# A later slot for the normalisations of the second mixing stage in a decoder layer on one NeuronCore

## The chip, the core and the metric

The kernel runs on one core of a Trainium2 chip, as a single launch. The metric is the device time of one execution in microseconds (us). The engines are TensorE (PE, with its weight loads shown apart as PEld), VectorE (DVE), ScalarE (ACT), GpSimd (POOL) and the queue of SyncE (SP). Each executes its own instructions in order and waits for the others on semaphores.

## The reference, cut to what matters

The layer is self-attention, a cross-attention block that mixes along the sequence (an attention-free transformer with a local bias), and a quantised feed-forward network, over x of shape (4, 1024, 512) in float32. The change lies in the second half of the cross block, from the weighted sums to the first layer norm:

```
def _aft_local(emb, wq, bq, wk, bk, wv, bv, wo, bo, pos_bias):
    ...
    num = jnp.einsum('tj,bjd->btd', ew, ek * v)
    den = jnp.einsum('tj,bjd->btd', ew, ek)
    y = jax.nn.sigmoid(q) * num / den
    return y @ wo + bo
...
attn = _aft_local(emb, wq, bq, wk, bk, wv, bv, wo, bo, pos_bias)
a = _layer_norm(attn + emb, gamma, beta)
```

with `_layer_norm(x) = (x - mu) * rsqrt(var + 1e-5) * gamma + beta` over the last axis of 512.

## The kernel before, in words

The layer is written as six stages one after the other, each with its own memory and semaphores: `project_qkv`, `attend`, `mix_in`, `mix_out`, `cross_ffn`, `quantised_ffn`. The change touches only `mix_out`, the second mixing stage, which the trace shows from about 1905 to 2275 us.

`mix_out` goes over B = 4 batches ("blocks"), each of T = 1024 tokens in TB = 8 tiles of 128 rows. A block is worked in 8 slots, `for s in range(TB)`, and every engine has a `body(b, first, more)` that lists what it does in each slot. The first and the last block are written out, the two between are a loop. In slot s:

- TensorE turns the y of two slots ago (`turn_y`, L1637), turns one of the two parts of a tile of exponentials two tiles ahead (`turn_e`, L1619), makes the denominator and the numerator of tile s (`weigh`, L1652 for the far part and L1658 for the near one; called den and num), turns the second part, and multiplies the y of tile s-2 by the output weights (`out_product`, L1681). Each product is split in high and low parts. In slot 7 it also turns the sums of the next block (L1628), ahead of the out product.
- ScalarE copies the turned tiles into their high parts (`round_y` L1728, `round_e` L1715 and L1716).
- GpSimd makes the low parts of the exponentials (`split_e`, L1567, two in a slot). A finished half is multiplied by gamma and shifted by beta there as well (`scale_and_shift`, L1575 and L1577, a pair for each of its four tiles), and its store to `a_rows` is issued from there (L1581).
- VectorE makes the low part of y (`split_y`, L1762), then `divide` (L1770, the reciprocal L1773, y itself L1776), then the `residual` of tile s-3 (L1788) and its statistics (L1790).

A half is four tiles, so a block has two: half 0 is tiles 0 to 3, half 1 tiles 4 to 7. The residual of a half's last tile comes in slot 6 (half 0) and in slot 2 of the next block (half 1). It is followed by the means and variances (L1795), the reciprocal square roots in 14 small instructions on all four tiles together (lines 114 to 119), and the four normalisations in place, `(z - mean) * rstd` (L1802). The last half of all has a path of its own (`finish_last`). After the last block two more slots (8 and 9) drain the out products, and slot 10 the last residual.

The accumulator has four banks in a ring. `free_bank` says what each product waits for before it writes its bank: den of slot s takes the bank that the out product of slot s-2 wrote, and that one is read by the residual of slot s-1.

```
                        for kind in ("den", "num"):
                            weigh(b, s, kind)
                        if ahead:
                            turn_e(*ahead, 1)
                        if more and s == TB - 1:
                            turn_sums(b + 1)
                        if not (first and s < LAG):
                            out_product(b, s)
```

The diff's functions are printed here.

Of the kernel before, what the change touches and what calls it, by code (L numbers as in the profile page):

```python
# [27 lines left out]
ALU = mybir.AluOpType  # L28
# [4 lines left out]
B, T, D = 4, 1024, 512  # L33
# [6 lines left out]
HT = HALF // P  # L40
# [29 lines left out]
def past(engine, sem, value):  # L70

    if not (isinstance(value, int) and value <= 0):
        engine.wait_ge(sem, value)


def half_of(rows, n):

    return rows.rearrange("(n t p) d -> n p t d", p=P, t=HT)[bass.ds(n, 1)].rearrange("a p t d -> p (a t) d")
# [7 lines left out]
def row(vector, start, n):  # L86

    return vector[start:start + n].rearrange("(a n) -> a n", a=1).to_broadcast([P, n])
# [1310 lines left out]
def mix_out(nc, ident, ewT_parts, e0_rows, wo, gamma, beta, emb_rows, expq_rows, ek_cols, ekv_cols, sum_cols, a_rows):  # L1399
# [11 lines left out]
    ACC, LAG = 4, 2  # L1411
    AHEAD = 2
    STEPS = 2 * HT + RSQRT_STEPS
    with ExitStack() as ctx:
# [22 lines left out]
        z = sb("z", [P, 2, HT, D])  # L1437
        w_raw = z[:, 0]
        stats = sb("stats", [P, HT, 6])
        moments = sb("moments", [P, HT, 2])  # L1440
        rstd = sb("rstd", [P, HT])
# [26 lines left out]
        norm_ready = sem("norm_ready")  # L1468
# [15 lines left out]
        def bank_of(kind, t):  # L1484

            step = t + (LAG if kind == "out" else 0)
            return (len(KINDS) * step + KINDS.index(kind)) % ACC
# [7 lines left out]
        with nc.Block() as block:  # L1495
# [50 lines left out]
            @block.gpsimd  # L1546
            def _(pool):
                pool.dma_start(gamma_row[:, :], row(gamma, 0, D)).then_inc(rows_loaded, 16)
                pool.dma_start(beta_row[:, :], row(beta, 0, D)).then_inc(rows_loaded, 16)

                pool.memset(zero[:, :], 0.0).then_inc(setup_step, 1)
                pool.memset(sums_wide[:, :, :, :, :], 0.0).then_inc(setup_step, 1)
                pool.wait_ge(setup_step, 2)

                def widen_sums(b):

                    pool.wait_ge(sums_loaded, (b + 1) * 16)
                    past(pool, sums_turned, b * 2)
                    for i in range(3):
                        pool.tensor_tensor(sums_wide[:, :, :, i, 0:TB], sums_in[:, :, :, :], zero[:, :].to_broadcast([P, 2 * KB * TB])  # L1560
                                           .rearrange("p (i c t) -> p i c t", i=2, c=KB), ALU.add).then_inc(sums_copied, 1)

                def split_e(b, t, i):
                    k = (b * TB + t) * 2 + i + 1
                    pool.wait_ge(e_full_ready, k)
                    pool.wait_ge(e_hi_ready, k)
                    pool.tensor_tensor(e_lo[:, t, i], e_full[:, i], e_hi[:, t, i].bitcast(F32), ALU.subtract).then_inc(e_lo_ready, 1)  # L1567

                def scale_and_shift(b, h, tiles):

                    n = b * 2 + h
                    for t in tiles:
                        i = n * HT + t
                        pool.wait_ge(norm_ready, i + 1)
                        pool.tensor_tensor(z[:, h, t], z[:, h, t], gamma_row[:, :], ALU.mult).then_inc(scaled, 1)  # L1575
                        pool.wait_ge(scaled, i + 1)
                        pool.tensor_tensor(z[:, h, t], z[:, h, t], beta_row[:, :], ALU.add).then_inc(shifted, 1)  # L1577
                    if HT - 1 in tiles:
                        pool.wait_ge(shifted, (n + 1) * HT)
                        pool.sem_inc(wait_taken, 1)  # L1580
                        pool.dma_start(half_of(a_rows, n), z[:, h]).then_inc(stored[h], 16)  # L1581

                def body(b, first, more):
                    for s in range(TB):
                        ahead = block_ahead(b, s, more)
                        if ahead:
                            split_e(*ahead, 0)
                            split_e(*ahead, 1)

                        if s == 0 and not first:  # L1590
                            scale_and_shift(b - 1, 0, range(2, HT))
                        if s in (3, 4) and not first:
                            scale_and_shift(b - 1, 1, range(2 * (s - 3), 2 * (s - 2)))
                        if s == 5 and more:
                            widen_sums(b + 1)
                        if s == 7:
                            scale_and_shift(b, 0, range(2))

                widen_sums(0)
                for t in range(2):  # L1600
                    for i in range(2):
                        split_e(0, t, i)
                pool.wait_ge(rows_loaded, 32)
                sequences(pool, body)
                scale_and_shift(B - 1, 0, range(2, HT))
                pool.wait_ge(norm_ready, N // P)
                pool.sem_inc(wait_taken, 1)
                pool.dma_start(half_of(a_rows, 2 * B - 1), z[:, 1]).then_inc(stored[1], 16)
                for h in range(2):
                    pool.wait_ge(stored[h], B * 16)  # L1610
# [142 lines left out]
            def _(dve):  # L1753
# [10 lines left out]
                def divide(b, t):  # L1764

                    i = b * TB + t
                    dve.wait_ge(expq_loaded[t % 4], (b * 2 + t // 4 + 1) * 16)
                    past(dve, read["num"], i)
                    dve.wait_ge(ready["den"], i + 1)
                    dve.scalar_tensor_tensor(out=recip[:, :], in0=expq_in[:, t % 4], scalar=1.0, in1=acc[:, bank_of("den", t)],  # L1770
                                             op0=ALU.add, op1=ALU.mult).then_inc(read["den"], 1)
                    dve.wait_ge(read["den"], i + 1)
                    dve.reciprocal(recip[:, :], recip[:, :]).then_inc(recip_step, 1)  # L1773
                    dve.wait_ge(recip_step, i + 1)
                    dve.wait_ge(ready["num"], i + 1)
                    dve.tensor_tensor(y[:, t % 4], acc[:, bank_of("num", t)], recip[:, :], ALU.mult).then_inc(read["num"], 1)  # L1776

                def residual(b, t):

                    if t < 0:  # L1780
                        b, t = b - 1, t + TB
                    i, h, k = b * TB + t, t // HT, t % HT
                    s0 = (b * 2 + h) * STEPS
                    if k == 0:
                        past(dve, stored[h], b * 16)
                    dve.wait_ge(emb_loaded[t % 4], (b * 2 + t // 4 + 1) * 16)
                    dve.wait_ge(ready["out"], i + 1)
                    dve.tensor_tensor(z[:, h, k], acc[:, bank_of("out", t)], emb_in[:, t % 4], ALU.add).then_inc(read["out"], 1)  # L1788
                    dve.wait_ge(read["out"], i + 1)
                    dve.bn_stats(stats[:, k], z[:, h, k]).then_inc(stat_step, 1)  # L1790
                    if k == HT - 1:
                        dve.wait_ge(stat_step, s0 + HT)
                        dve.sem_inc(wait_taken, 1)
                        for j in range(HT):
                            dve.bn_aggr(moments[:, j], stats[:, j]).then_inc(stat_step, 1)  # L1795
                        dve.wait_ge(stat_step, s0 + 2 * HT)
                        rsqrt(dve, moments[:, :, 1], rstd[:, :], nt_half[:, :], nt_square[:, :], stat_step, s0 + 2 * HT)
                        if isinstance(i, int) and i == N // P - 1:
                            finish_last(h)
                        else:  # L1800
                            for j in range(HT):
                                dve.tensor_scalar(z[:, h, j], z[:, h, j], moments[:, j, 0:1], rstd[:, j:j + 1],  # L1802
                                                  ALU.subtract, ALU.mult).then_inc(norm_ready, 1)

                def finish_last(h):

# [8 lines left out]
                def body(b, first, more):  # L1815
                    for s in range(TB):
                        if not (first and s < LAG):
                            split_y(b, s - LAG)
                        if first and s == 1:
                            dve.wait_ge(w_hi_ready, 1)  # L1820
                            dve.tensor_tensor(w_lo[:, :, :], w_raw, w_hi[:, :, :].bitcast(F32), ALU.subtract).then_inc(w_lo_ready, 1)
                        divide(b, s)
                        if more and s == TB - 1:
                            split_sums(b + 1)
                        if not (first and s <= LAG):
                            residual(b, s - LAG - 1)
# [842 lines left out]
```

## Time and profile before

| what | value |
|---|---|
| median of 3 runs | 3545.81 us (3543.29 to 3549.79) |
| the profiled execution's own time | 3542.34 us |
| its span | 3540.7 us |
| TensorE busy | 3167.0 us, 89% of the span |
| VectorE busy | 2344.0 us, 66% |
| ScalarE busy | 1767.6 us, 50% |
| GpSimd busy | 1171.8 us, 33% |

The profile is of one execution. Its span is the time from the first to the last instruction that it shows; the execution's own time holds the launch around it too. A busy share is an average over all six stages, so what a change in one stage is worth is read from that stage. Start times are in us from the start of the span.

### The profile page before, as it was taken

The numbers are of one execution on the slowest core, as the hardware profiler recorded it, in microseconds if no ns is written. First come the engines' busy times: TensorE is split into PE (matmuls) and PEld (weight loads), VectorE is DVE, ScalarE is ACT, GpSimd is POOL, SyncE is SP. The second block draws the span as 40 slices with busy tenths as digits, with TensorE's granted clock in tenths as the row PEclk, the third lists the DMA queues.
The fourth block names the chain that finished last, engine by engine and source line by source line (L and its number), as shares of the span: only waits on it lengthen the run. The fifth ranks groups of instructions, "written<-read, shape, count | busy, mean of one in ns | idle before, by whom it ended". The sixth has DMA issues, their size and how long they took to land. (4 is left out here: it accounts for less than half of the span.)

```text
span 3540.7 us, 57138 instructions
## 1 busy us (share of the span) xinstructions
PE 3167.0 (89%) x19234; PEld 2282.3 (64%) x19234; DVE 2344.0 (66%) x4197; ACT 1767.6 (50%) x3130; POOL 1171.8 (33%) x901
## 2 busy tenths in 40 slices
PE   6998999999999999789996998599999999368886
PEld 5776666666666666567775777487877788334443
DVE  5562788888888888644553888634445444379996
ACT  3331888888888888522323222132222222076662
POOL 2343311312231132144442455300111111058886
PEclk9999999999999999999998999799999999689999
DMA  6775311321222122355645443321111110201112
GB/s 216 239 243 169 85 60 56 92 62 56 73 79 61 56 85 68 122 181 188 228 171 184 129 131 118 108 84 42 42 42 43 42 42 29 82 22 55 60 42 72
DMA packets 239351, 350.53 MB, mean 99 GB/s; under 512 B 31792, under 2 KB 129104, under 8 KB 239184
## 3 DMA queue, kind: packets, MB, share of 16 engines
q1 hardware_dynamic: 208256, 290.41, 25.5%
q0 software_dynamic: 8912, 32.82, 2.8%
q10 hardware_dynamic: 22016, 25.17, 2.0%
q8 instruction: 93, 1.52, 0.2%
q14 instruction: 74, 0.61, 0.1%
HBM read 210.68 MB, written 137.64 MB: 98 GB/s over the span
## 5 line engine op out<-in xcount | busy, mean ns | idle before, releaser
L887 DVE CUSTOM_DVE_ANT_0 attend_scores<-attend_scores,attend_bias_table 128x1024 f32<-128x1024 f32 x512 | 630.5, 1232 | 164.8 <-PE attend_scores L741 161.5
L814 ACT ACTIVATE attend_probs<-attend_scores,attend_neg_max 128x1024 f32<-128x1024 f32 x512 | 571.7, 1117 | 141.0 <-DVE attend_neg_max L887 131.3
L753 PE MATMUL attend_turned<-ident,attend_probs 128*128 128x128 f32 x4096 | 557.3, 275 | 12.6 <-DVE attend_probsT L895 12.5
L753 PEld LDWEIGHTS attend_turned<-ident,attend_probs 128*128 128x128 f32 x4096 | 472.9, 141 | 121.4 <-DVE attend_probsT L895 30.2
L741 PE MATMUL attend_scores<-attend_k_stack,attend_q_stack 96*128 96x512 f32 x1024 | 373.4, 446 | 18.1 <-DMA attend_q_stack<-qk_parts 15.0
L822 ACT COPY attend_probsT<-attend_turned 128x512 f32<-128x512 f32 x640 | 359.5, 583 | 24.7 <-PE attend_turned L753 23.1
L2217 DVE TENSOR_TENSOR cross_ffn_h_lo<-cross_ffn_hidden,cross_ffn_h_hi 128x512 fp32r<-128x512 f32 x128 | 95.8, 753 | 363.7 <-ACT cross_ffn_h_hi L2114 363.1
L703 POOL TENSOR_TENSOR attend_out_parts<-attend_out_full,attend_out_parts 128x256 fp32r<-128x256 f32 x64 | 46.6, 727 | 847.3 <-ACT attend_out_parts L829 847.3
L768 PE MATMUL attend_out_acc<-attend_probsT,attend_v_in 128*32 128x256 f32 x4096 | 312.9, 389 | 0.7 <-DVE attend_out_full L905 0.7
L741 PEld LDWEIGHTS attend_scores<-attend_k_stack,attend_q_stack 96*128 96x128 f32 x1024 | 154.1, 190 | 175.2 <-issue 154.8
L895 DVE COPY attend_probsT<-attend_turned 128x512 f32<-128x512 f32 x384 | 263.5, 686 | 1.3 <-PE attend_turned L753 1.3
L2111 ACT ACTIVATE cross_ffn_hidden<-cross_ffn_h_acc,cross_ffn_b_cols 128x512 f32<-128x512 f32 x128 | 88.2, 689 | 266.3 <-PE cross_ffn_h_acc L2028 250.1
L697 POOL TENSOR_TENSOR attend_bias_table<-attend_neg_distance,attend_slope_now 128x1920 f32<-128x1920 f32 x64 | 214.8, 3388 | 1.4
L2026 PE MATMUL cross_ffn_h_acc<-cross_ffn_aT_hi,cross_ffn_w_hi 128*128 128x512 f32 x512 | 203.6, 398 | 5.6 <-issue 5.6
L2375 POOL TENSOR_TENSOR quantised_ffn_conv<-quantised_ffn_conv,quantised_ffn_right_tap 128x512 f32<-128x512 f32 x128 | 178.4, 1394 | 88.8 <-DVE quantised_ffn_conv L2543 88.8
L2039 PE MATMUL cross_ffn_out_acc<-cross_ffn_w_hi,cross_ffn_h_hi 128*128 128x512 f32 x512 | 206.3, 403 | 1.1 <-DVE cross_ffn_h_lo L2217 0.6
L2027 PE MATMUL cross_ffn_h_acc<-cross_ffn_aT_hi,cross_ffn_w_lo 128*128 128x512 f32 x512 | 202.9, 396 | 0.0
L2114 ACT CAST cross_ffn_h_hi<-cross_ffn_hidden 128x512 fp32r<-128x512 f32 x128 | 79.5, 621 | 247.1 <-PE cross_ffn_out_acc L2041 246.1
L2028 PE MATMUL cross_ffn_h_acc<-cross_ffn_aT_lo,cross_ffn_w_hi 128*128 128x512 f32 x512 | 202.5, 396 | 0.0
L2040 PE MATMUL cross_ffn_out_acc<-cross_ffn_w_lo,cross_ffn_h_hi 128*128 128x512 f32 x512 | 202.3, 395 | 0.0
L2041 PE MATMUL cross_ffn_out_acc<-cross_ffn_w_hi,cross_ffn_h_lo 128*128 128x512 f32 x512 | 202.3, 395 | 0.0
L2381 POOL TENSOR_TENSOR quantised_ffn_h_scaled<-quantised_ffn_h,quantised_ffn_scale_row 128x512 f32<-128x512 f32 x128 | 164.2, 1285 | 12.3 <-ACT quantised_ffn_scale_row L2513 7.6
(294 smaller groups left out, 6644.5 us busy)
## 6 DMA issues: line engine op xcount, KB each, us to landing
qk_parts<-qkv_qk_out SPq DMA_DIRECT2D x64, 512.0 KB, 3.2
attend_k_stack<-qk_parts SPq DMA_DIRECT2D x192, 128.0 KB, 2.5
attend_q_stack<-qk_parts SPq DMA_DIRECT2D x192, 128.0 KB, 2.7
qkv_wq_raw<-L_ffn_w POOLq DMA_DIRECT2D x16, 1024.0 KB, 7.6
o_parts<-attend_out_parts ACTq DMA_DIRECT2D x64, 256.0 KB, 2.5
carried_o_in<-o_parts SPq DMA_DIRECT2D x32, 512.0 KB, 6.5
qkv_x_in<-x SPq DMA_DIRECT2D x8, 1024.0 KB, 5.7
v_rows<-qkv_v_out SPq DMA_DIRECT2D x32, 256.0 KB, 3.4
```

The lines of the kernel that those rows point to most:

```text
L697: pool.tensor_tensor(bias_table[:, h], neg_distance[:, :], slope_now[:, h:h + 1].to_broadcast([P, SPAN]), ALU.mult).then_inc(table_ready, 1)
L741: last = pe.matmul(scores[:, i % 2, k * HALF:(k + 1) * HALF], q_stack[:, h, queries], k_stack[:, h, k * HALF:(k + 1) * HALF], start=True, ...
L753: last = pe.transpose(turned[:, x, c], probs[:, i % 2, k * P:(k + 1) * P], ident[:, :])
L768: last = pe.matmul(out_acc[rows, 0:QG], v_in[:, c, rows], probsT[:, (qg - 1) % 2, c, h], start=(c == 0), stop=(c == TB - 1))
L814: act.activation(probs[:, i % 2], scores[:, i % 2], ACT.Exp, bias=neg_max[:, i % 4:i % 4 + 1], scale=-1.0, accum_out=den[:, qg % 2, j, h:h ...
L822: act.copy(probsT[:, qg % 2, x * HB:(x + 1) * HB, h, j * P:(j + 1) * P], turned[:, x]).then_inc(copied[x], 1)
L887: dve.tensor_tensor_reduce(scores[:, i % 2], scores[:, i % 2], bias_table[:, h, at:at + T], -1.0, BIG, ALU.add, ALU.min, neg_max[:, i % 4: ...
L895: dve.tensor_copy(probsT[:, qg % 2, HB:TB, h, j * P:(j + 1) * P], turned[:, 1]).then_inc(copied[1], 1)
L2026: pe.matmul(out, w1_hi[:, c, cols], aT_hi[:, c], start=c == 0, stop=False)
L2027: pe.matmul(out, w1_lo[:, c, cols], aT_hi[:, c], start=False, stop=False)
L2028: last = pe.matmul(out, w1_hi[:, c, cols], aT_lo[:, c], start=False, stop=c == KB - 1)
L2039: pe.matmul(out_acc[:, t], hi, w2_hi[:, j], start=j == 0, stop=False)
```

## The change

Three things move inside `mix_out`; no instruction is added or taken out, and no tile changes its size.

- VectorE: the four normalisations of a half leave `residual` and become `normalise(h)`. It is called a slot later, after `divide` and before the residual: in slot 7 for half 0 (`HT + LAG + 1`), in slot 3 of the next block for half 1 (`LAG + 1`).
- GpSimd: the scale and shift of half 0 is done two tiles in slot 0 and two in slot 1 of the next block (before: two in slot 7 and two in slot 0), that of half 1 in slots 4 and 5 (before: 3 and 4). The store of a half follows its last pair. After the last block all four tiles of half 0 are done in one go (before: two).
- GpSimd: the sums of the next block are widened in slot 6 (before: slot 5).

```
@@ gpsimd, body @@
-                        if s == 0 and not first:
-                            scale_and_shift(b - 1, 0, range(2, HT))
-                        if s in (3, 4) and not first:
-                            scale_and_shift(b - 1, 1, range(2 * (s - 3), 2 * (s - 2)))
-                        if s == 5 and more:
+                        if s in (0, 1) and not first:
+                            scale_and_shift(b - 1, 0, range(2 * s, 2 * s + 2))
+                        if s in (4, 5) and not first:
+                            scale_and_shift(b - 1, 1, range(2 * (s - 4), 2 * (s - 3)))
+                        if s == 6 and more:
                             widen_sums(b + 1)
-                        if s == 7:
-                            scale_and_shift(b, 0, range(2))
...
-                scale_and_shift(B - 1, 0, range(2, HT))
+                scale_and_shift(B - 1, 0, range(HT))
@@ vector, residual @@
                         if isinstance(i, int) and i == N // P - 1:
                             finish_last(h)
-                        else:
-                            for j in range(HT):
-                                dve.tensor_scalar(z[:, h, j], z[:, h, j], moments[:, j, 0:1], rstd[:, j:j + 1],
-                                                  ALU.subtract, ALU.mult).then_inc(norm_ready, 1)
+
+                def normalise(h):
+
+                    for j in range(HT):
+                        dve.tensor_scalar(z[:, h, j], z[:, h, j], moments[:, j, 0:1], rstd[:, j:j + 1],
+                                          ALU.subtract, ALU.mult).then_inc(norm_ready, 1)
@@ vector, body @@
                         divide(b, s)
+                        if s == HT + LAG + 1:
+                            normalise(0)
+                        if s == LAG + 1 and not first:
+                            normalise(1)
                         if more and s == TB - 1:
                             split_sums(b + 1)
                         if not (first and s <= LAG):
                             residual(b, s - LAG - 1)
```

## Rows read from the trace of the kernel before

**Rows 1.** The page: busy time of each engine, share of the span, instructions.

```profile
PE 3167.0 (89%) x19234; PEld 2282.3 (64%) x19234; DVE 2344.0 (66%) x4197; ACT 1767.6 (50%) x3130; POOL 1171.8 (33%) x901
```

**Rows 2.** Waits of TensorE, 1925 to 2275 us: who for whom, us, times, longest.

```profile
PE mix_out_acc L1681 <- DVE mix_out_yT_lo L1762: 25.2, 9, 4.9
PE mix_out_acc L1652 <- DVE mix_out_z L1788: 7.8, 6, 1.5
```

**Rows 3.** Timeline of TensorE, a block's end: start, us, instruction [idle before it].

```profile
2087.27 0.50 PE L1681 MATMUL mix_out_acc<-mix_out_w_hi,mix_out_yT_hi 128*128 128x512 f32 x1 [3.98 <-DVE mix_out_yT_lo L1762]
...
2091.73 0.60 PE L1637 MATMUL mix_out_turned<-ident,mix_out_y 128*128 128x128 f32 x4
...
2094.21 0.47 PE L1652 MATMUL mix_out_acc<-mix_out_sums,mix_out_e_stack 96*128 96x512 f32 x1 [1.45 <-DVE mix_out_z L1788]
```

**Rows 4.** Timeline of TensorE, a block's middle, and den of its slot 6.

```profile
2126.08 0.50 PE L1681 MATMUL mix_out_acc<-mix_out_w_hi,mix_out_yT_hi 128*128 128x512 f32 x1 [1.63 <-DVE mix_out_yT_lo L1762]
...
2128.98 0.60 PE L1637 MATMUL mix_out_turned<-ident,mix_out_y 128*128 128x128 f32 x4
...
2131.39 0.50 PE L1652 MATMUL mix_out_acc<-mix_out_sums,mix_out_e_stack 96*128 96x512 f32 x1 [1.37 <-DVE mix_out_z L1788]
...
2148.95 0.48 PE L1652 MATMUL mix_out_acc<-mix_out_sums,mix_out_e_stack 96*128 96x512 f32 x1
```

**Rows 5.** Timeline of VectorE: a block's end, a block's middle, the last block's end.

```profile
2082.77 3.85 DVE L1802 TENSOR_SCALAR mix_out_z<-mix_out_z,mix_out_moments,mix_out_rstd 128x512 f32<-128x512 f32 x4
...
2091.24 0.69 DVE L1776 TENSOR_TENSOR mix_out_y<-mix_out_acc,mix_out_recip 128x512 f32<-128x512 f32 x1
...
2123.52 1.91 DVE L1802 TENSOR_SCALAR mix_out_z<-mix_out_z,mix_out_moments,mix_out_rstd 128x512 f32<-128x512 f32 x4
2125.35 0.68 DVE L1762 TENSOR_TENSOR mix_out_yT_lo<-mix_out_turned,mix_out_yT_hi 128x512 fp32r<-128x512 f32 x1
...
2130.66 0.68 DVE L1788 TENSOR_TENSOR mix_out_z<-mix_out_acc,mix_out_emb_in 128x512 f32<-128x512 f32 x1
...
2240.12 3.80 DVE L1802 TENSOR_SCALAR mix_out_z<-mix_out_z,mix_out_moments,mix_out_rstd 128x512 f32<-128x512 f32 x4
```

**Rows 6.** Timeline of GpSimd: a split in slot 0, two behind a store.

```profile
2094.17 1.29 POOL L1567 TENSOR_TENSOR mix_out_e_lo<-mix_out_e_full,mix_out_e_hi 128x512 fp32r<-128x512 f32 x1 [3.84 <-ACT mix_out_e_hi L1716]
...
2146.13 2.55 POOL L1567 TENSOR_TENSOR mix_out_e_lo<-mix_out_e_full,mix_out_e_hi 128x512 fp32r<-128x512 f32 x2
```

**Rows 7.** Instructions of L1802: ns minimum, median, maximum; first and last start.

```profile
L1802 DVE TENSOR_SCALAR mix_out_z<-mix_out_z,mix_out_moments,mix_out_rstd x28: 539/546/1530, 2003.3 to 2242.4; 128x512 f32<-128x512 f32 x28
```

**Rows 8.** Windows: length, busy per engine, granted clock of PE, DMA share, GB/s.

```profile
2083.00:2093.00 10.00, 5.78 (x23) 4.28 (x21) 9.90 (x10) 2.06 (x6) 6.50 (x5) 0.83 0.00 0
3156.00:3164.00 8.00, 4.62 (x24) 2.48 (x25) 7.05 (x14) 5.26 (x11) 4.36 (x4) 1.00 0.01 2
3252.00:3260.00 8.00, 6.51 (x34) 3.54 (x35) 7.97 (x15) 5.27 (x11) 4.86 (x4) 1.00 0.21 68
3301.00:3309.00 8.00, 6.03 (x23) 3.20 (x24) 6.42 (x13) 3.70 (x7) 3.19 (x4) 0.79 0.21 66
1531.00:1537.00 6.00, 5.84 (x18) 4.69 (x19) 5.58 (x16) 0.69 (x1) 2.93 (x3) 0.69 0.38 129
```

**Rows 9.** Timeline of TensorE: gaps in three stages (the number in brackets).

```profile
1531.15 0.77 PE L1186 MATMUL mix_in_acc<-mix_in_eT_hi,mix_in_wk_hi 128*128 128x512 f32 x1 [6.40 <-DVE mix_in_x L1329]
...
2251.20 0.50 PE L1681 MATMUL mix_out_acc<-mix_out_w_hi,mix_out_yT_hi 128*128 128x512 f32 x1 [1.58 <-DVE mix_out_yT_lo L1762]
...
3157.93 0.63 PE L2420 MATMUL quantised_ffn_turned<-ident,quantised_ffn_h 128*128 128x128 f32 x4 [3.09 <-DVE quantised_ffn_block_max L2551]
...
3206.14 0.63 PE L2420 MATMUL quantised_ffn_turned<-ident,quantised_ffn_h 128*128 128x128 f32 x4 [3.60 <-DVE quantised_ffn_block_max L2551]
...
3302.97 1.09 PE L2420 MATMUL quantised_ffn_turned<-ident,quantised_ffn_h 128*128 128x128 f32 x4 [3.60 <-DVE quantised_ffn_block_max L2551]
...
3449.37 0.83 PE L2420 MATMUL quantised_ffn_turned<-ident,quantised_ffn_h 128*128 128x128 f32 x4 [3.60 <-DVE quantised_ffn_block_max L2551]
```

## The prediction

> **What bounds the kernel now.** I read the page first: TensorE (PE) is busy 3167.0 of 3540.7 us [rows 1], so a stage can gain only where PE stands still in it. Next come PE's waits in the second mixing stage, 1925 to 2275 us: the largest is the out product (L1681) held for y's low part from DVE (L1762), 25.2 us in 9 waits; the next that recurs is the first weigh product of a slot (L1652) held for the residual (L1788), 7.8 us in 6 waits [rows 2]. Third, the timelines of PE and DVE show that both sit where a half is normalised. I follow one block end and one block middle; the first, second and third blocks have such an end, the second to fourth such a middle, and the last half 0 (in the last block's slot 7) runs into the stage's tail.
>
> *Block end (slot 7, half 0).* PE waits 3.98 us, starts the out product at 2087.27, turns y for the next slot at 2091.73, waits 1.45 us and starts den(0) at 2094.21 [rows 3]. *Block middle (slot 3, half 1).* 1.63 us of wait, out product at 2126.08, turn at 2128.98, 1.37 us, den(4) at 2131.39 [rows 4]. DVE is idle in neither: it ends its reciprocal square roots and runs the four normalisations, split_y, divide and the residual without a break [rows 5]. So DVE's queue from the square roots to the residual of the next slot sets when den(0) and den(4) may start. In the code this is free_bank: den of slot s writes the bank that out of slot s-2 held, which the residual of slot s-1 on DVE reads.
>
> **The change, part by part.**
>
> *Normalisations moved behind divide.* They stay ahead of the residual of the same slot. Call the square roots' end R. Before: R, four normalisations, split_y, divide, residual, den. After: R, split_y, divide, four normalisations, residual, den. The same instructions stand between R and den. The out product does start earlier: split_y begins at R instead of R+1.83 (2123.52 to 2125.35) in the middle, and instead of R+3.77 at a block end (the four last 3.85 there against 1.91, and the next instruction starts 0.08 before they end) [rows 5]. PE starts 0.73 behind split_y's start (2125.35 to 2126.08 [rows 4, 5]), so at a block end at 2082.77+0.73=2083.5, where it was ready at 2087.27-3.98=2083.29. But PE then only comes sooner to den and waits there for the same residual. I book nothing for the wait that goes: what is late next is den. The wait becomes one piece. At a block end the out product (2.90 us at full clock, 2126.08 to 2128.98 [rows 4]) ends at 2086.4, the turns take 1.04 (2131.39-1.37-2128.98), and PE stands from 2087.4 until den. In the middle PE was ready for the out product at 2126.08-1.63=2124.45, so it turns at 2127.35 and stands from 2128.4 until den, 3.0 us if den stays at 2131.39.
>
> *What the normalisations cost in their new place.* Four take 1.83 us until the next starts where GpSimd is quiet, 3.77 where it works [rows 5]; one takes 0.55 us, up to 1.53 if a GpSimd instruction runs [rows 7]. At a block end today two of four are hit, once by GpSimd's second split and once by its scale, which the first normalisation itself sets off. After the change the scale is a slot away, but one split remains: GpSimd's first split starts 2.44 us behind the turn (2094.17-2091.73 [rows 3, 6]), so at 2086.4+2.44=2088.8 and lasts 1.3 [rows 6]. The normalisations start behind y: 2091.24-3.77+0.7=2088.2, and run until 2090.0. One of them falls under it: +0.87, near the 1.53-0.55=0.98 that a whole hit costs and a little less, since it is already due when the split starts. Per block end: -1.94+0.87=-1.07. Bounds: -1.94 (missed) and 0 (two hit). In the middle they were free of it; now they run from 2130.66-1.83=2128.8 to 2130.7 and the split is due at 2127.35+2.44=2129.8, so the fourth is hit: +0.6, bounds 0 and +0.98. Sum: 3 x -1.07 + 3 x 0.6 = -1.4 us.
>
> The Trainium skill, "SBUF — State Buffer", section "Who interferes with whom", says of this that issue order decides who blocks, and that the loser blocks for the whole instruction. The trace agrees: 1.53 against 0.55 us [rows 7]. By a rule of whole instructions the block end could lose all of today's 1.94 or keep half of it, which are the bounds already taken.
>
> *TensorE's clock.* Where a gap of PE is long, the granted clock behind it falls from 2.4 to 1.2 GHz. Over 2083 to 2093 it is 0.83, 1.7 us of full clock lost in 10 [rows 8], and the out product took 4.46 us (2087.27 to 2091.73) instead of 2.90. Today this costs nothing, as den waits for the residual anyway (1.45 us left over). After the change the gap lies in front of den, and what follows is den, num and out of a slot that PE paces: whatever is lost there is paid. Where does it fall? Behind 3.98 us it does [rows 3, 8]. In the last stage a gap of 3.09 us leaves it at 1.00; of the six of 3.60 to 3.62 us (the first at 3206.14, the last at 3449.37) five have 0.79 in the 8 us around them, as the one at 3302.97 (1.7 us lost), and one has 1.00 (3252 to 3260) [rows 8, 9]. In front of the first mixing stage's products, behind 6.40 us, it is 0.69 over 6 us: 1.9 us [rows 8, 9]. The new gaps: block end 2087.4 to 2094.21-1.07=2093.1, 5.7 us, falls, 1.8 us each (between 1.7 and 1.9), +5.4. Middle 3.0+0.6=3.6 us, falls five times in six, 1.7 each, +5.1. The bounds of one fall are 0 and 1.9 us.
>
> The Trainium skill, "TensorE: Matmul & The Clock Gate", Part 1, states that an idle PE is throttled and that activity releases it; this speaks against a change that gathers two short waits into a long one. Rows 8 and 9 agree, and the sum is made from them.
>
> *The tail.* In the last block's slot 7 GpSimd has no split; its scales start behind the first normalisation as now, so two of four are hit and R to out product 8 stays the same 11.08 us (2240.12 to 2251.20 [rows 5, 9]), with the same instructions of DVE between them. Out product 7 starts at 2240.12+0.73=2240.85, ends at 2243.75, the turn of y(6) takes to 2244.2, and PE stands 7 us until out product 8. That one ran at full clock, behind a 1.58 us gap; now it falls: +1.8 (bounds 0 and 1.9), on the path to the last residual.
>
> *GpSimd's new deal.* Scale and shift is the same work, in slots 0, 1, 4, 5 instead of 7, 0, 3, 4; the store goes at the end of slots 1 and 5. The splits behind a store today run back to back and end at 2148.68 (2146.13+2.55), 0.27 us ahead of the den that needs them, at 2148.95 [rows 4, 6], and PE does not wait. The new pairs at slots 1 and 5 put the same row of work ahead of den(3) and den(7) at the same slot length: I book 0, with 0.27 us of cover each; bounds 0 and 1. The half's store has to land before the residual of slots 3 and 7 writes the tile: the store leaves near the start of slots 2 and 6, over 12 us ahead. The widening moves behind slot 6's splits and so ends about when den(7) starts; PE turns the sums only behind den and num of slot 7, some 3 us later: 0. The store of the last first half leaves some 5 us later, and still lands before the last store is issued, behind the last half's own square roots and normalisations: 0. SP's loads are not moved.
>
> **Sum.** -1.4 (sharing) +5.4 (block ends' clock) +5.1 (middles' clock) +1.8 (tail) = +10.9 us. The profiled execution took 3542.34 us (span 3540.7 and 1.6 around it), 3.5 below the median, so 3553.2 on its own scale; on the median 3545.8+10.9=3556.7.
>
> **Rivals.**
> - *Forecast: the long gaps cost clock*, all seven. 3556.7, own range 3553 to 3559 (seven times 1.5 to 1.9, sharing -3.2 to 0). Chance 0.50.
> - *The middles keep their clock*: the split misses the normalisations or the gap stays near 3.09. -1.4+5.4+1.8=+5.8, less 1.8 if missed: 3550 to 3552. For it: 3.6 is at the edge of the rows. Chance 0.22.
> - *The clock is not paid at all*, because it has come back before den, or falls within the gap only. Sharing alone: -1.4, and -5.8 if no split hits. 3540 to 3544.5. Against it: 0.69 behind 6.40 us. Chance 0.10.
> - *Faster: the waits for y's low part do go*. That needs den(0) and den(4) not to wait for the residual of the slot before; then up to some 22 of the 25.2 us come back: 3524. It decides at free_bank. For it: those waits are the largest. Against: the six waits L1652 for L1788, present in every event even after a late out product. Chance 0.09.
> - *GpSimd becomes late*: if its splits in slots 2 and 6 end over 0.27 us later than the pattern at 2148.68, den(3) and den(7) wait. One us later costs 0.7 in six places, +4 on the forecast: 3561. Chance 0.09.
>
> About 0.2% (7.1 us) is what a measurement of this kernel can tell from no change. Faster: 0.09. Same: 0.33 (the third case, most of the second, the forecast's low edge). Slower: 0.58. The range of 3541 to 3563 leaves out the faster case and the end of the last.
>
> **What the profile after would show.** Right: the wait of L1681 for L1762 shrinks from 25.2 to about 10 us, 7 of it in the tail, and that of L1652 for L1788 grows from 7.8 to about 28, with single waits of 3.6 and 5.7; the four normalisations last 2.5 to 2.9 us; the granted clock is under 0.85 in the 8 us from den(0) and den(4); den follows R by 10.4 us at block ends (11.4 now) and 8.5 in the middle (7.9 now). Wrong: den's wait stays under 2 us (the faster rival); full clock behind the gaps; or PE waits for GpSimd's e_lo.

## The result and the profile after

| | before | after |
|---|---|---|
| median of 8 runs | 3543.86 us (3540.98 to 3549.79) | 3558.34 us (3555.84 to 3562.22) |
| span of the profiled execution | 3540.7 us | 3560.3 us |

The change makes the kernel slower, by little but clear of the noise: ratio 1.0041, 95% interval 1.003 to 1.0051, so 14.5 us with bounds of about 10.6 and 18.1. 3556.7 was forecast. The profiled execution of after took 3562.21 us, next to the longest of its eight, so the spans exaggerate the difference. What the stage itself lost is read inside the traces, from the start of the out product of slot 6 in the first block, ahead of the first moved instruction, to the first turn of the next stage: 2282.40-1995.20=287.2 us before, 2297.33-1998.05=299.3 after, 12.1 more. Of the 19.6 us between the two spans 2.9 lie ahead of this stretch and 4.7 behind it.

TensorE's waits in the stage (1925 to 2295 us; waiting line, releaser, total, times, longest) answer to [rows 2]. Lines moved up by two: the out product is L1679, the first weigh product L1650, split_y L1760, the residual L1786.

```profile
PE mix_out_acc L1650 <- DVE mix_out_z L1786: 29.5, 6, 5.8
...
PE mix_out_acc L1679 <- DVE mix_out_yT_lo L1760: 10.6, 7, 6.8
```

The wait that the change aimed at did shrink, from 25.2 to 10.6 us, and 6.84 of what is left is one wait in the tail. But the wait of den for the residual grew from 7.8 to 29.5. Together they went from 33.0 to 40.1 us. TensorE's timeline at the same three places (block end, block middle, tail) answers to [rows 3, 4, 9]:

```profile
2091.24 0.50 PE L1679 MATMUL mix_out_acc<-mix_out_w_hi,mix_out_yT_hi 128*128 128x512 f32 x1 [0.23 <-DVE mix_out_yT_lo L1760]
...
2094.14 0.60 PE L1635 MATMUL mix_out_turned<-ident,mix_out_y 128*128 128x128 f32 x4
...
2100.95 0.77 PE L1650 MATMUL mix_out_acc<-mix_out_sums,mix_out_e_stack 96*128 96x512 f32 x1 [5.77 <-DVE mix_out_z L1786]
...
2135.23 0.60 PE L1635 MATMUL mix_out_turned<-ident,mix_out_y 128*128 128x128 f32 x4
...
2140.42 0.50 PE L1650 MATMUL mix_out_acc<-mix_out_sums,mix_out_e_stack 96*128 96x512 f32 x1 [4.15 <-DVE mix_out_z L1786]
...
2264.82 0.80 PE L1679 MATMUL mix_out_acc<-mix_out_w_hi,mix_out_yT_hi 128*128 128x512 f32 x1 [6.84 <-DVE mix_out_yT_lo L1760]
```

Two waits, 3.98 and 1.45 us at a block end and 1.63 and 1.37 in a middle, have become one, of 5.77 and 4.15. VectorE's timeline beside it, as in [rows 5], shows that its queue is as full as before:

```profile
2090.49 0.69 DVE L1760 TENSOR_TENSOR mix_out_yT_lo<-mix_out_turned,mix_out_yT_hi 128x512 fp32r<-128x512 f32 x1
...
2095.81 2.85 DVE L1802 TENSOR_SCALAR mix_out_z<-mix_out_z,mix_out_moments,mix_out_rstd 128x512 f32<-128x512 f32 x4
2098.69 1.29 DVE L1756 TENSOR_TENSOR mix_out_sums<-mix_out_sum_acc,mix_out_sums 32x512 fp32r<-32x512 f32 x2
2100.02 0.69 DVE L1786 TENSOR_TENSOR mix_out_z<-mix_out_acc,mix_out_emb_in 128x512 f32<-128x512 f32 x1
...
2131.59 0.69 DVE L1760 TENSOR_TENSOR mix_out_yT_lo<-mix_out_turned,mix_out_yT_hi 128x512 fp32r<-128x512 f32 x1
...
2136.91 2.85 DVE L1802 TENSOR_SCALAR mix_out_z<-mix_out_z,mix_out_moments,mix_out_rstd 128x512 f32<-128x512 f32 x4
2139.68 0.68 DVE L1786 TENSOR_TENSOR mix_out_z<-mix_out_acc,mix_out_emb_in 128x512 f32<-128x512 f32 x1
```

From the end of the square roots (the start of split_y) den follows after 2100.95-2090.49=10.46 us at a block end (11.44 before) and 2140.42-2131.59=8.83 in the middle (7.87 before). The four normalisations last 2.85 us at both places, where they lasted 3.85 and 1.91. GpSimd's timeline shows the instruction that lengthens them, a split that starts 0.8 us into them, and the two splits behind a store:

```profile
2096.60 1.32 POOL L1567 TENSOR_TENSOR mix_out_e_lo<-mix_out_e_full,mix_out_e_hi 128x512 fp32r<-128x512 f32 x1 [3.91 <-ACT mix_out_e_hi L1714]
...
2124.38 2.55 POOL L1567 TENSOR_TENSOR mix_out_e_lo<-mix_out_e_full,mix_out_e_hi 128x512 fp32r<-128x512 f32 x2
```

Last, windows of 10 us from the product behind each long wait (length, busy time of each engine, granted clock, DMA), as in [rows 8]: a middle, a block end, a middle, the tail.

```profile
2057.30:2067.30 10.00, 9.95 (x34) 7.97 (x35) 6.49 (x6) 1.07 (x2) 0.79 (x1) 0.72 0.38 105
2100.90:2110.90 10.00, 9.95 (x43) 8.26 (x44) 7.72 (x8) 2.40 (x5) 3.33 (x3) 0.85 0.43 109
2140.40:2150.40 10.00, 9.98 (x41) 8.04 (x42) 7.30 (x7) 1.07 (x2) 1.83 (x2) 0.83 0.36 105
...
2264.80:2274.80 10.00, 7.89 (x28) 5.88 (x28) 3.83 (x6) 0.58 (x1) 6.32 (x6) 0.85 0.24 91
```

In all four TensorE is at 1.2 GHz for a part of the window and busy almost throughout it in the first three: 10 x (1-0.85)=1.5 to 10 x (1-0.72)=2.8 us of work are lost. The other three falls give 0.73 (the first block end), 0.85 and 0.83. In the kernel before, the same windows, from den(0) and from den(4) on, are at full clock:

```profile
2094.20:2104.20 10.00, 9.99 (x49) 8.30 (x50) 7.71 (x8) 2.66 (x5) 5.98 (x5) 1.00 0.49 147
2131.40:2141.40 10.00, 10.00 (x49) 8.27 (x50) 7.97 (x8) 2.44 (x5) 5.33 (x5) 1.00 0.44 126
```

There the fall behind the 3.98 us ends within the out product, ahead of a den that waits for the residual in any case.

### The profile page after: what moved, and what is told of

Read it like the earlier page. It is cut to its first block and busy times, and to the rows that moved or that the text cites. A ratio compares the mean times of both kernels' runs of the same rounds, so it can differ in the third digit from the quotient of the medians.

```text
span 3560.3 us, 57119 instructions
## 1 busy us (share of the span) xinstructions
PE 3181.3 (89%) x19208; PEld 2290.8 (64%) x19234; DVE 2344.4 (66%) x4197; ACT 1766.4 (50%) x3130; POOL 1170.5 (33%) x901
## 5 line engine op out<-in xcount | busy, mean ns | idle before, releaser
L741 PE MATMUL attend_scores<-attend_k_stack,attend_q_stack 96*128 96x512 f32 x1024 | 372.5, 445 | 17.6 <-DMA attend_q_stack<-qk_parts 14.5
L2385 POOL TENSOR_TENSOR quantised_ffn_h_scaled<-quantised_ffn_h,quantised_ffn_scale_row 128x512 f32<-128x512 f32 x128 | 164.8, 1290 | 12.2 <-ACT quantised_ffn_scale_row L2517 7.5
```

The lines of the kernel that those rows point to most:

```text
L741: last = pe.matmul(scores[:, i % 2, k * HALF:(k + 1) * HALF], q_stack[:, h, queries], k_stack[:, h, k * HALF:(k + 1) * HALF], start=True, ...
```

## The experiments

The theory: what starts den is the residual of the slot before on VectorE, the normalisations stay in its way, GpSimd's split makes them longer, and the long gap costs clock. Seven kernels were run, each against the kernel before. "Stage" is the stretch defined above, in the one execution of each kernel that was profiled; how much it scatters between executions was not measured.

| kernel | start, end of the stage, us | stage | against before | median, runs | ratio to before, 95% |
|---|---|---|---|---|---|
| before | 1995.20, 2282.40 | 287.2 | | | |
| after | 1998.05, 2297.33 | 299.3 | +12.1 | 3558.34, 8 | 1.0041 (1.003 to 1.0051) |
| e1 VectorE's part alone | 1995.60, 2303.57 | 308.0 | +20.8 | 3564.11, 5 | 1.0058 (1.0044 to 1.0072) |
| e2 GpSimd's part alone | 1995.48, 2280.67 | 285.2 | -2.0 | 3539.49, 11 | 0.9989 (0.998 to 0.9998) |
| e3 behind the residual | 1996.52, 2270.46 | 273.9 | -13.3 | 3533.74, 7 | 0.9973 (0.9961 to 0.9984) |
| e4 gaps filled | 1997.41, 2292.62 | 295.2 | +8.0 | 3555.7, 5 | 1.0036 (1.0022 to 1.0049) |
| e5 dealt over two slots | 1992.86, 2267.87 | 275.0 | -12.2 | 3529.67, 5 | 0.9959 (0.9946 to 0.9973) |
| e6 numerator first | 1998.40, 2269.39 | 271.0 | -16.2 | 3527.3, 5 | 0.9952 (0.9939 to 0.9966) |
| e7 after, numerator first | 1997.24, 2288.55 | 291.3 | +4.1 | 3547.24, 11 | 1.001 (1.0001 to 1.0019) |

e1 to e4 ran on one chip, beside a kernel before of 3544.45 us; e5 to e7 on one, beside one of 3544.35.

### e1: VectorE's part alone

The kernel after with GpSimd's lines as they were before (the line behind the last block too):

```
-                        if s in (0, 1) and not first:
-                            scale_and_shift(b - 1, 0, range(2 * s, 2 * s + 2))
-                        if s in (4, 5) and not first:
-                            scale_and_shift(b - 1, 1, range(2 * (s - 4), 2 * (s - 3)))
-                        if s == 6 and more:
+                        if s == 0 and not first:
+                            scale_and_shift(b - 1, 0, range(2, HT))
+                        if s in (3, 4) and not first:
+                            scale_and_shift(b - 1, 1, range(2 * (s - 3), 2 * (s - 2)))
+                        if s == 5 and more:
                             widen_sums(b + 1)
+                        if s == 7:
+                            scale_and_shift(b, 0, range(2))
```

> The kernel after, with GpSimd's old deal put back (scale and shift in slots 7, 0, 3, 4, widening in slot 5); only VectorE's normalisations are moved. Theory (the residual in front of den sets the end, sharing with GpSimd lengthens the normalisations, and the long gap costs clock): GpSimd now chases the normalisations with its scale in slots 7 and 3, so four of them last about 3.8 us at both places instead of 2.85. PE waits for L1786 grow to some 6.7 us at a block end and 5.1 us in the middle; the loss against the kernel before is about 19 us (3563). Rival A (GpSimd's new deal, its later store or splits cause a good part of the loss): the loss is smaller than the 14.5 us of the whole change, near 7 us or less. Rival B (the moved normalisations cost nothing by themselves): no difference from before.

Measured: 19.7 us above before. TensorE's waits of e1, then VectorE's normalisations at a block end and in a middle (timeline):

```profile
PE mix_out_acc L1652 <- DVE mix_out_z L1788: 35.2, 6, 6.7
```

```profile
2094.28 3.80 DVE L1804 TENSOR_SCALAR mix_out_z<-mix_out_z,mix_out_moments,mix_out_rstd 128x512 f32<-128x512 f32 x4
...
2137.10 3.80 DVE L1804 TENSOR_SCALAR mix_out_z<-mix_out_z,mix_out_moments,mix_out_rstd 128x512 f32<-128x512 f32 x4
```

They last 3.80 us at both places, since the first of them sets GpSimd's scale and shift off beside the others, and den's waits are 6.72 and 5.08 us. So the whole loss, and more, sits in VectorE's part, and GpSimd's new deal takes 8.7 us of it back in the stage (308.0 to 299.3). Rival A, that GpSimd's new deal costs, is out, and so is rival B.

### e2: GpSimd's part alone

The kernel before with the diff of e1 read the other way (slots 0, 1, 4 and 5, widening in slot 6); VectorE as before.

> The kernel before, with GpSimd's new deal alone (slots 0, 1, 4, 5, widening in slot 6); the normalisations stay where they were. Theory: the scale no longer hits the normalisations at a block end, only a split does, so they last about 2.85 us instead of 3.85, the wait ahead of the out product falls from 4.0 to about 3.0 us and its clock stays up; den(0) comes 1 us earlier three times: 3 us faster than before (3541), the middles unchanged. The splits behind a store still end ahead of their den, so no PE wait for e_lo. Rival A (the new deal makes GpSimd late): PE shows waits for e_lo in slots 3 and 7 and the time is 4 us or more above before.

Measured: ratio 0.9989, 5 us by the medians and 2.0 in the stage; its interval just leaves out 1. From out product to out product, each of the three block ends (slot 4 to slot 0) is 0.95 us shorter than before, which is the 3 us expected, the middles are unchanged, and the tail is 0.8 longer. VectorE's timeline at a block end, TensorE's waits, and two windows, of the block end with both its gaps and of the 10 us from den(0) on:

```profile
2082.11 2.90 DVE L1800 TENSOR_SCALAR mix_out_z<-mix_out_z,mix_out_moments,mix_out_rstd 128x512 f32<-128x512 f32 x4
```

```profile
PE mix_out_acc L1679 <- DVE mix_out_yT_lo L1760: 22.2, 9, 4.9
PE mix_out_acc L1650 <- DVE mix_out_z L1786: 11.6, 5, 3.0
```

```profile
2085.60:2092.60 7.00, 3.94 (x20) 3.14 (x21) 6.83 (x8) 1.60 (x3) 1.26 (x1) 1.00 0.00 0
2092.60:2102.60 10.00, 10.00 (x49) 8.28 (x50) 7.70 (x8) 2.66 (x5) 4.72 (x4) 1.00 0.49 147
```

One of the four is still hit, by the split, and no longer two: 2.90 us for 3.85. With the scale a slot away the wait ahead of the out product is 3.04 us and the clock stays at 1.00, where it had been 0.83 over 10 us. The tail lost its 0.8 us to the clock: ahead of the out product of slot 7 the wait is 4.93 us for 4.94, but the granted clock is 0.60 over the 7.6 us from there to the next out product, where it was 0.75 over 6.7. GpSimd is not late: TensorE shows no wait for e_lo between 1960 and 2262 us, in e2 as in after.

### e3: the normalisations behind the residual

The diff is against the kernel after.

```
                         divide(b, s)
-                        if s == HT + LAG + 1:
-                            normalise(0)
-                        if s == LAG + 1 and not first:
-                            normalise(1)
                         if more and s == TB - 1:
                             split_sums(b + 1)
                         if not (first and s <= LAG):
                             residual(b, s - LAG - 1)
+                        if s == HT + LAG + 1 and more:
+                            normalise(0)
+                        if s == LAG + 1 and not first:
+                            normalise(1)
...
                     residual(B - 1, s - LAG - 1)
+                    if s == TB:
+                        normalise(0)
```

> The kernel after, with the normalisations one place further back: behind the residual of slots 7 and 3 (for the last half 0 behind the residual of slot 8), all else the same. Theory (den waits for that residual, whose queue held the normalisations): den(0) starts about 7.7 us behind the end of the square roots instead of 10.5, den(4) 6.0 instead of 8.9; gaps of PE stay near 3 us or less and the clock stays up. Part comes back as a wait of the next slot's den, up to 1.7 us at a block end and about 1 us in the middle, since VectorE has only some 2 us of slack a slot. Against before: 1.7 us at each of 3 block ends, 0.7 to 1.6 in 3 middles, 2 in the tail, about 10 us faster (3534); against after about 25 us. Rival (den is held by something else than the residual, as GpSimd or y): den stays where it is in the kernel after and the time stays near 3558.

Measured: 10.7 us faster than before, 25 faster than after, as expected. TensorE's timeline at a block end of e3:

```profile
2083.83 0.60 PE L1635 MATMUL mix_out_turned<-ident,mix_out_y 128*128 128x128 f32 x4
...
2087.86 0.47 PE L1650 MATMUL mix_out_acc<-mix_out_sums,mix_out_e_stack 96*128 96x512 f32 x1 [3.00 <-DVE mix_out_z L1786]
```

Den starts 2.8 us sooner behind the turn than in after (4.0 for 6.8 us), which is the length of the normalisations. That is the direct test of what holds den: only the order on VectorE was changed. Against before, the block ends are 2.2, 2.0 and 2.0 us shorter, the middles 2.0, 1.9 and 1.6 and the tail 1.7, most of them a little more than expected. The way in which part was to come back was wrong, though. I expected a wait of the next slot's den, and there is none (six waits of L1650 for L1786 in all, the six that were there). What came back is clock, behind a gap that I had taken for short enough; windows of 10 us behind den(0) and behind den(4):

```profile
2087.90:2097.90 10.00, 10.00 (x43) 8.15 (x44) 9.39 (x12) 2.28 (x5) 3.21 (x3) 0.83 0.42 118
...
2124.70:2134.70 10.00, 9.99 (x49) 8.14 (x50) 9.90 (x12) 2.43 (x5) 4.58 (x4) 1.00 0.39 107
```

### e4: the gaps filled

The kernel after, with products that nobody reads in TensorE's long gaps (17 ahead of den(4), 28 ahead of the out product of slot 8). No output depends on them.

```
+                def fill(n):
+                    for _ in range(n):
+                        pe.matmul(sum_acc[:, 0], w_hi[:, 0, 0:P], w_hi[:, 0], start=True, stop=True)
...
+                        if s == HT and not first:
+                            fill(17)
                         for kind in ("den", "num"):
                             weigh(b, s, kind)
...
+                    if s == TB:
+                        fill(28)
                     out_product(B - 1, s)
```

> The kernel after, with 17 products of 128x512 whose result nobody reads put in TensorE's gap ahead of den(4) of the second to fourth block, and 28 of them ahead of the out product of slot 8; they write the bank of the turned sums, which is free there. Nothing else changes, VectorE's order neither. Theory (the clock falls behind those gaps and what is lost is paid): the granted clock stays at 1.00 behind them, each middle gives back 1.7 to 2.2 us and the tail 1.3, so 6 to 8 us faster than the kernel after (3551); the three block ends keep their fall. Rival (the loss in the middles is the longer normalisations and what they delay, and the slow clock is hidden by other waits): no gain, or 1 us of loss, against the kernel after.

Measured: 4.1 us less than after in the stage, not 6 to 8. The medians are 2.6 apart, with intervals that overlap, so this reading rests on the traces. Windows of 10 us of e4, from a middle and from two block ends:

```profile
2057.00:2067.00 10.00, 9.96 (x49) 8.26 (x50) 8.01 (x8) 2.40 (x5) 3.26 (x3) 1.00 0.41 125
2098.00:2108.00 10.00, 9.90 (x37) 7.99 (x38) 7.20 (x7) 1.07 (x2) 2.05 (x2) 0.70 0.40 107
...
2179.70:2189.70 10.00, 9.95 (x36) 7.91 (x37) 7.31 (x7) 1.07 (x2) 1.95 (x2) 0.69 0.34 105
```

At the places that were filled the theory holds: the clock is at 1.00, and from the out product of slot 0 to that of slot 4, where only the gap ahead of den(4) differs, e4 takes 2.5, 1.5 and 1.65 us less than after (39.73 for 42.24, 39.54 for 41.08, 40.03 for 41.68 us), the tail 1.4 less. That is 7.1 us. Den(4) itself starts no sooner: in the second middle, 34.4 us behind the out product of slot 0 in both kernels. What came back is the clock behind it. But the block ends, which were not filled, took 0.3, 1.3 and 1.4 us more than in after, with the same gaps of 5.77, 5.77 and 5.58 us: their falls are longer, 0.70, 0.70 and 0.69 where after has 0.73, 0.85 and 0.85. So the cost of a fall is not set by its gap alone. What sets it is not shown; the first block end lies ahead of every gap that was filled.

### e5: the normalisations dealt over two slots

The diff is against e3; behind the last block all four are still done in one go.

```
                        if s == HT + LAG + 1 and more:
-                            normalise(0)
+                            normalise(0, range(2))
+                        if s == 0 and not first:
+                            normalise(0, range(2, HT))
                        if s == LAG + 1 and not first:
-                            normalise(1)
+                            normalise(1, range(2))
+                        if s == LAG + 2 and not first:
+                            normalise(1, range(2, HT))
```

> e3 with a half's four normalisations dealt over two slots behind the residual: two in slot 7 and two in slot 0 of the next block (half 0), two in slot 3 and two in slot 4 (half 1). In e3 PE waits at a block end 3.0 us ahead of den(0), and the granted clock falls to 0.83 over the next 10 us. Theory (what is left in e3 is the square roots ahead of den and the clock that falls behind the gap, not the normalisations): dealing them changes neither, so the time is that of e3, 3534, within 2 us; the gap stays at 3.0 us and the clock falls as before. Rival (VectorE's queue behind the residual is what came back in e3): 1 us is won at each of six places, 3528.

Measured: 14.7 us below before, where e3 was 10.7 below it. By the medians that is nearer to the rival, though the two intervals overlap. The trace speaks for the theory: in the stage e5 is 1.1 us longer than e3, the wait ahead of den(0) is 3.00 us again, and the clock over 2084 to 2094 us is 0.83 again. The profiled execution of e5 took 4.9 us less than that of e3: 3.7 of them lie ahead of the stage and 2.3 behind it, where the two kernels are the same, and the stage gives 1.1 back. That the medians differ for such a reason is likely and not shown.

### e6: the numerator ahead of the denominator

The diff is against e5, cut to TensorE's body.

```
+                        swapped = s in (0, HT) and not first
-                        for kind in ("den", "num"):
-                            weigh(b, s, kind)
+                        for kind in ("num", "den") if swapped else ("den", "num"):
+                            weigh(b, s, kind, swapped)
```

In `weigh` a swapped product begins with its near parts and ends with the part of the sums; the wait for the split sums stands right ahead of that. All else is e5.

> e5, and in slots 0 and 4 TensorE makes the numerator ahead of the denominator, near products first and the one of the sums last: the numerator's bank is free long before, so real work stands in the gap. Theory (the gap ahead of den is idle time that other work can fill, and with it the clock stays up): the granted clock behind a block end is 1.00, and the next limit is the residual of slots 0 and 4 that den of slots 1 and 5 wait for, so 1.4 us is won at each block end and 1.3 in each middle against e3, 8 us in all (3526). Rival (order of products does not matter, since VectorE gates every slot there): the time of e3, 3534.

Measured: 17 us below before. The median is 2.4 us below that of e5, with intervals that overlap; the stage is 4.0 shorter. TensorE's waits of e6 between 1960 and 2262 us, and a window behind a block end:

```profile
PE mix_out_acc L1651 <- DVE mix_out_z L1793: 8.6, 7, 1.5
...
PE mix_out_acc L1662 <- DVE mix_out_sums L1763: 2.1, 3, 0.7
PE mix_out_acc L1657 <- DVE mix_out_z L1793: 0.7, 3, 0.2
```

```profile
2087.50:2097.50 10.00, 8.35 (x39) 6.44 (x40) 9.83 (x13) 2.66 (x5) 6.12 (x6) 1.00 0.42 117
```

Real work stands in the gap, the clock does not fall, and at a block end TensorE waits 0.7 us for the sums and 0.2 for the residual instead of 3.0. Now VectorE is busy 9.83 of 10 us and the next slot's den waits 1.4 us for it: of the 8 us expected against e3, the stage shows 2.9 (270.99 for 273.94). From the out product of slot 5 to that of slot 1 of the next block, so across a block end, e6 takes 1.5, 1.2 and 1.0 us less than e3, near the 1.4 expected. From slot 1 to slot 5, across a middle, it wins next to nothing (0.04, 0.05 and -0.12) where 1.3 was expected: the 1.37 us that den(4) waited in e3 are waited by den(5) instead. From the last of these out products to the end of the stage it takes 0.8 more, the clock in the tail being 0.83 over 2235.8 to 2245.8 us where e3 has 1.00.

### e7: the kernel after with that order alone

> The kernel after, with TensorE's order of e6 in slots 0 and 4 as its only edit; VectorE keeps its normalisations ahead of the residual. Theory: den still starts 8.9 (middle) and 10.5 us (block end) behind the square roots, but the gap holds the numerator; in the middle it shrinks from 4.1 to about 1.8 us and the clock stays up, at a block end from 5.8 to some 4.4, where the clock may still fall. Den of slots 1 and 5 then waits for its residual. About 2 us is won in six places: 12 us faster than the kernel after (3546). Rival (the clock and the gap are not what costs, the residual's place alone is): no more than 2 us.

Its only edit against the kernel after is the order of e6. Measured: 11.1 us less than after by the medians, 8.0 in the stage, ratio to before 1.001 (1.0001 to 1.0019). TensorE's waits between 1960 and 2262 us, and windows of 10 us behind a middle and a block end:

```profile
PE mix_out_acc L1662 <- DVE mix_out_sums L1763: 10.4, 3, 3.5
```

```profile
2055.40:2065.40 10.00, 8.57 (x42) 6.92 (x43) 7.90 (x8) 2.66 (x5) 5.50 (x5) 1.00 0.41 123
2094.90:2104.90 10.00, 8.62 (x34) 6.66 (x35) 7.88 (x8) 2.66 (x5) 4.00 (x4) 0.83 0.39 105
```

With VectorE's order unchanged, most of the loss goes when the gap ahead of den is used, and in the middle, where the gap shrinks from 4.15 to 1.82 us, the clock stays up. At a block end the numerator in its turn waits 3.46 us for the sums that VectorE splits behind the normalisations, and the clock is 0.71, 0.83 and 0.67. So most of the loss of the change was idle time and slow clock ahead of and behind den, which the place of the normalisations brings only as long as TensorE has nothing else to do there. The order alone was not run on the kernel before. How much of the 8.0 us it would win there too is open; on e5 it won 4.0.

## Why the prediction was right

*The normalisations moved, at nothing gained.* Right. Of 3.98 us ahead of the out product 0.23 stayed, and den's wait rose from 1.45 to 5.77 us. e3 shows by the order alone that the residual is what den waits for.

*What they cost in their new place.* Right at a block end: 10.46 us from square roots to den, 10.4 forecast. In the middle the term was +0.6 and measured +0.96 (8.83 for 7.87): the split hits one whole normalisation there too, 2.85 for 1.91 us, so the gap is 4.15 us and not 3.6. It was the bound of +0.98 that came in. Sum of the six: 3 x -0.98 + 3 x 0.96 = -0.1 us, where -1.4 was booked. By the rule of whole instructions that the prediction draws on, a block end keeps half of its 1.94, so it wins 0.97 us. The prediction calls that a bound already taken, which it is not (they were -1.94 and 0), but it is what was measured.

*The clock.* Right in place and number, seven falls. The sum books all three middles in full (3 x 1.7 = 5.1), though the text gives each of them only five chances in six, which would make 4.25. The price of the falls was put at 1.7 to 1.8 us each and 12.3 in all; the windows give 2.7, 1.5 and 1.5 at block ends (0.73, 0.85, 0.85), 2.8, 1.7 and 1.7 in middles, 1.5 in the tail: 13.4. Seen from the out products, the block ends took 1.5, 0.4 and 0.4 us more than before, the middles 3.4, 2.5 and 2.9, all as the intervals from slot 4 to slot 0 and from slot 0 to slot 4, and the tail, from the out product of slot 4 to the end of the stage, 1.1: 12.1 together. Windows and sharing make 13.4 - 0.1 = 13.3, so 1.2 more than the out products show; that is not accounted for singly. In the middles e4 tells the two terms apart: with the clock 2.5, 1.5 and 1.65 us come back, which leaves 0.9, 0.9 and 1.2 for the later den, where 0.96 was measured directly.

*The tail* lost 1.1 us for 1.8 forecast: its wait of 6.84 us and its fall are as described, but the fall ended within the out product, which took 1.3 us longer (4.23 for 2.90).

*GpSimd's new deal at 0.* Right: the splits end at 2124.38+2.55=2126.93 and TensorE has no wait for e_lo. The 0.95 us that e2 wins at each block end by itself is the hit of the scale that is gone, which the prediction books under the normalisations' cost.

*The size.* The stage is 12.1 us longer against 10.9 forecast. The medians differ by 14.5, with an interval that reaches down to 10.6; that the other 2.4 us is scatter between executions is likely and not shown. Some luck is in it: the forecast of 3556.7 lies 1.6 us from the measured 3558.34, but it starts from a median of three runs, 3545.8, that is 1.9 above that of eight, 3543.86. As a difference it missed by 3.6 us.

## What to carry to other kernels

Before an instruction is moved past another on a full queue, look for the next thing that the same queue releases: here the wait only moved from the out product to den, since everything between the square roots and the residual was still done first. Two short waits of TensorE are not the same as one long one. Behind the long ones here, 4.13 to 6.84 us, the clock was low each time, and it fell on work that TensorE paces; in the kernel before, a fall of the same kind lay ahead of a wait and cost nothing. The order that pays puts the residual that frees a bank first and the normalisations, which nobody waits for yet, behind it, and lets TensorE begin with the product whose bank is already free: e6, in which the normalisations are also dealt over two slots, is 17 us faster than the kernel before and 31 faster than the change.

## What the hardware showed that I had not expected

The length of a gap does not settle whether the clock falls near 3 us. In the last stage of the kernel before a gap of 3.09 us left it at 1.00 [rows 8, 9]; in e2 den waits 3.00 us behind an out product and the clock stays at 1.00 in the 10 us that follow; in e3 and e5 the same 3.00 us ahead of the same product were followed by 0.83. Even a much shorter wait can be followed by a fall. In e2 the out product of slot 3 in the second block starts behind 1.86 us of wait and runs for the most part at 1.2 GHz, as this window shows; in the kernel before, the clock behind the same 1.86 us is 1.00 (2046.8 to 2052 us):

```profile
2046.20:2056.20 10.00, 9.99 (x40) 8.07 (x41) 8.49 (x8) 1.66 (x3) 1.96 (x2) 0.83 0.35 100
```

That fall cost nothing either: from the out product of slot 0 to that of slot 4 e2 takes 38.87 us there and the kernel before 38.86, since den(4) no longer waits its 1.37 us. And the price of a fall varies: behind the same wait of 5.77 us, 2.7 us were lost at the first block end of after and 1.5 at the second, and 3.0 at both in e4.
